# A megakernel's mixing stage: partition halves that hold row pairs, a projection in 64x64 quarters, one residual sum a pair, and x1 in DRAM at a padded channel pitch

## What is computed

```python
# layer 0
y = gn(x)                                  # group norm, 16 groups
qkv = dwconv3x3(conv1x1(y))                # 144 channels
q, k, v = blocks(qkv)                      # 8 heads x 96 rows (6 channels x 4x4 sites) x 16384 tokens
attn = softmax(normalise(q) @ normalise(k).T * temperature)   # 96 x 96 a head
x1 = x + proj(from_blocks(attn @ v))       # proj: 48x48, 1x1 conv
# layer 1: four recurrent sweeps (down, up, right, left), each step
#   next = line + conv1d_5(carry) + bias
out = x1 + sweeps(gn(x1))
```

## Time and profile before

| What | Value |
|---|---|
| median of 3 runs | 10475.02 us (10473.13 to 10499.15) |
| span of the profiled execution, first to last instruction | 10449.6 us |
| granted TensorE clock, mean | 0.956 |
| busy, share of the span: PE, PEld, DVE, ACT, POOL | 90%, 87%, 77%, 61%, 29% |
| mixing, first group's store to last group's store | 4142.0 to 5260.9 us |
| final sum, first to last addition | 9754.0 to 10435.6 us |

### The profile page before, as it was taken

The page is one execution under the profiler, slowest core; times in us unless marked ns, Lnnn a source line. Parts: engine busy times, 40 slices in busy tenths (PEclk is TensorE's granted clock), DMA queues, the critical chain, the costliest instruction groups (busy, mean ns, idle before and its releaser), DMA issues. The chain is left out here.

```text
span 10449.6 us, 213663 instructions
## 1 busy us (share of the span) xinstructions
PE 9389.1 (90%) x72744; PEld 9047.4 (87%) x72744; DVE 8070.5 (77%) x16201; ACT 6339.0 (61%) x11047; POOL 2982.2 (29%) x4333
## 2 busy tenths in 40 slices
PE   2999999999999998999979999999999999999100
PEld 2999999999999998777779999999999999999100
DVE  7888888777777776998977777777799997777333
ACT  2777777767777775444456667999833336666100
POOL 0000000000000000000046666666666666666100
PEclk9999999999999998999989999999999999999555
DMA  8888887666666666999968887777766657777899
GB/s 246 166 167 164 167 166 144 125 125 130 133 129 133 132 131 127 270 266 256 267 156 198 199 202 185 211 217 214 208 209 213 220 194 190 198 197 204 346 431 406
DMA packets 740412, 2101.28 MB, mean 201 GB/s; under 512 B 58480, under 2 KB 633232, under 8 KB 649184
## 3 DMA queue, kind: packets, MB, share of 16 engines
q1 hardware_dynamic: 611920, 1744.17, 65.5%
q10 hardware_dynamic: 106368, 204.76, 6.1%
q0 software_dynamic: 22016, 151.01, 5.9%
HBM read 1344.51 MB, written 754.97 MB: 201 GB/s over the span
## 5 line engine op out<-in xcount | busy, mean ns | idle before, releaser
L1448 ACT CAST hi<-rough 112x256 fp32r<-112x256 f32 x4096 | 1666.8, 407 | 1410.8 <-DVE rough L1362 1359.8
L1282 PE MATMUL scan_ps<-hi,scan_high 112*112 112x256 f32 x12264 | 2125.0, 282 | 30.6 <-ACT hi L1448 30.6
L1362 DVE SCALAR_TENSOR_TENSOR rough<-scan_ps,scan_bias,lines 112x256 f32<-112x256 f32 x4086 | 2136.3, 523 | 19.0 <-issue 14.4
L1293 PE MATMUL scan_ps_low<-lo,scan_high 112*112 112x256 f32 x12264 | 2130.5, 282 | 1.1 <-POOL lo L1394 0.7
L1288 PE MATMUL scan_ps_low<-hi,scan_low 112*112 112x256 f32 x12264 | 2123.3, 281 | 0.0
L438 PE MATMUL conv_ps<-tap_high,x_high 128*128 128x432 f32 (+2 forms) x6144 | 1884.0, 307 | 27.6 <-DVE vt L645 15.7
L438 PE MATMUL conv_ps<-tap_low,x_high 128*128 128x432 f32 (+2 forms) x6144 | 1908.3, 311 | 0.0
L438 PE MATMUL conv_ps<-tap_high,x_low 128*128 128x432 f32 (+2 forms) x6144 | 1905.1, 310 | 0.0
L1282 PEld LDWEIGHTS scan_ps<-hi,scan_high 112*112 112x112 f32 x12264 | 1691.3, 175 | 32.1 <-ACT hi L1448 31.3
L1293 PEld LDWEIGHTS scan_ps_low<-lo,scan_high 112*112 112x112 f32 x12264 | 1684.7, 175 | 5.6 <-POOL lo L1394 2.8
L1288 PEld LDWEIGHTS scan_ps_low<-hi,scan_low 112*112 112x112 f32 x12264 | 1687.1, 176 | 0.0
(11 more groups left out here) (140 smaller groups left out, 12398.8 us busy)
## 6 DMA issues: line engine op xcount, KB each, us to landing
raw<-x SPq DMA_DIRECT2D x764, 256.0 KB, 5.3
d_rows<-lines SPq DMA_DIRECT2D x32, 3584.0 KB, 30.2
u_cols<-lines SPq DMA_DIRECT2D x64, 1792.0 KB, 13.3
r_cols<-lines SPq DMA_DIRECT2D x32, 3584.0 KB, 24.3
lines<-u_cols SPq DMA_DIRECT2D x31, 3584.0 KB, 16.5
lines<-r_cols SPq DMA_DIRECT2D x30, 3584.0 KB, 16.6
lines<-d_rows SPq DMA_DIRECT2D x30, 3360.0 KB, 15.6
v_blocks<-xs ACTq DMA_DIRECT2D x128, 768.0 KB, 5.6
```

Of the source, the lines that this page charges most:

```text
L1282: last = nc.tensor.matmul(ps[:, b, 0:LP], high[:, shift], hi[:, b, (k - 1) % 2, shift:shift + LP], start=shift == 0, stop=shift == 2)
L1293: last = nc.tensor.matmul(ps_low[:, b, 0:LP], high[:, shift], lo[:, b, shift:shift + LP], start=False, stop=shift == 2)
L1362: nc.vector.scalar_tensor_tensor(rough[:, b, k % 2], ps[:, b, 0:LP], bias, line(way, s, k % T, b, kept), ALU.add, ALU.add).then_inc(rough_ ...
L1448: nc.scalar.copy(hi[:, b, k % 2, 1:LP + 1], rough[:, b, k % 2]).then_inc(hi_ready[b], 1)
```

## The change

The turned pair of sites now lies differently. `attT` is permuted by a new constant matrix `order` (the 8 transposes of the setup become 8 matmuls with `order_sb`), so that the two partition halves of `turned` hold an upper and a lower row of one block (dy and dy + 2), at one column dx. For odd dx the two halves are swapped. A pair is now one row parity `low` and two columns.

- Project: instead of 2 matmuls of 112x112 with 512 moving, a pair takes 4 of 48 x 64 or 48 x 48, each on one half of the rows and one half of the output columns of the array. The fourth pair of a group is projected one block later than before (`project(1 - s if i else s, i - 1 if i else N - 1)`), and the group's last turn moves behind the next group's first products.
- Sum: `res` has the same halves, so one addition of 112 x 1024 takes the place of four of 48 x 512. The bn_stats come four after every second pair instead of two after each; their number and size stay.
- `res` is loaded in runs of 4 KiB instead of 16 KiB, `scan_t` stored in runs of 8 KiB instead of 16 KiB; bytes and number of DMAs stay. A memset of `res` takes the place of that of `scan_t`, and the first loads of `res` wait for it.
- x1_scan is `[B, C, PITCH]`, 1 MiB + 4 KiB a channel. The down sweep's tiles are loaded as before (16 KiB a partition, four DMAs), with rows in another order inside a tile (`x1_row`).
- Because of the pad, `final_sum` loads x1 by four DMAs of 32 partitions x 32 KiB (one channel each) instead of one of 128 partitions, and adds in 8 operations of 128 x 1024 instead of four of 128 x 2048.

```diff
+RUN = T * W
+PITCH = G * RUN + 1024
...
+def x1_groups(x1_scan, b):
+
+    return x1_scan[b, :, 0:G * RUN].rearrange("c (g q f t w) -> c g q f t w", g=G, q=2, f=2, t=NP)
+
+
+def x1_row(t):
+
+    return NP * (t % N // 2) + 2 * (t // N) + t % 2
...
-    x1_scan = dram("x1_scan", (B, C, G, 2, T, W2))
+    x1_scan = dram("x1_scan", (B, C, PITCH))
...
         def load_res(queue, b, g, s, half):
-            queue.dma_start(res[ODD * half:ODD * half + C, s],
-                            x[b, :, bass.ds(T * g + NP * half, NP)]).then_inc(res_landed[half][s], 16)
-
-        def store(queue, b, g, s, q):
+            rows = x[b].rearrange("c (g i f l) w -> c g i f (l w)", g=G, i=NB, f=2)
+            queue.dma_start(res[ODD * half:ODD * half + C, s].rearrange("p (i l) w -> p i (l w)", i=NB),
+                            rows[:, bass.ds(g, 1), :, half].rearrange("c g i lw -> c (g i) lw")).then_inc(res_landed[half][s], 16)
+
+        def store(queue, b, g, s, half):
 
             queue.wait_ge(summed, N * G * b + N * g + N)
-            queue.dma_start(x1_scan[b, :, bass.ds(g, 1), q].rearrange("c g t w -> c (g t) w"),
-                            scan_t[ODD * q:ODD * q + C, s]).then_inc(scan_out[q][s], 16)
+            queue.dma_start(x1_groups(x1_scan, b)[:, bass.ds(g, 1), :, half].rearrange("c g q t w -> c (g q) (t w)"),
+                            scan_t[ODD * half:ODD * half + C, s].rearrange("p q t w -> p q (t w)")).then_inc(scan_out[half][s], 16)
...
+                sp.wait_ge(res_clear, 1)
...
-                nc.gpsimd.memset(scan_t[:], 0.0).then_inc(scan_clear, 1)
+                nc.gpsimd.memset(res[:], 0.0).then_inc(res_clear, 1)
+                pool.wait_ge(res_clear, 1)
...
-                        last = nc.tensor.transpose(w_ps[:, h // 4, (h % 4) * HD:(h % 4 + 1) * HD], diag[:, h], eye[0:HD, 0:HD])
+                        last = nc.tensor.matmul(w_ps[:, h // 4, (h % 4) * HD:(h % 4 + 1) * HD], diag[:, h], order_sb[:],
+                                                start=True, stop=True)
...
-                def project(j, s, ms, first):
-                    for m in ms:
-                        if not (first and m < NBANK):
-
-                            pe.wait_ge(summed, N * j + m // 2 - 1)
-                        nc.tensor.matmul(o_ps[:, m % NBANK], projd[:], flat(turned[:, s, m]),
-                                         start=True, stop=True).then_inc(o_done, 1)
-
-                def turn(n, slot, first):
+                def project(s, pair):
+                    for m in (2 * pair, 2 * pair + 1):
+                        for half in range(2):
+                            to = half if m % 2 == 0 else 1 - half
+                            wide = C if to else ODD
+                            last = nc.tensor.matmul(o_ps[ODD * to:ODD * to + wide, m % NBANK],
+                                                    projd[ODD * half:ODD * half + C, 0:wide],
+                                                    flat(turned[ODD * half:ODD * half + C, s, m]), start=True, stop=True)
+                    last.then_inc(o_done, 1)
...
-                        if not first:
-                            if i == 0:
-                                if second:
-                                    pe.wait_ge(proj_in, 32)
-
-                                pe.wait_ge(turn_moved, n)
-                            project(j - 1, 1 - s, (2 * i, 2 * i + 1), second)
-                    turn(NB * j + NB - 1, (NB - 1) % 2, False)
...
+                def group(b, j, s):
+                    for i in range(NB):
+                        products(b, j, s, i)
+
+                        pe.wait_ge(summed, N * j + i - 6)
+                        turn(NB * j + i - 1, (i - 1) % 2)
+                        project(1 - s if i else s, i - 1 if i else N - 1)
...
+                    bank, low, col = 2 * (pair % 2), pair // 2, 2 * (pair % 2)
+                    v.wait_ge(o_done, N * j + pair + 1)
+                    nc.vector.tensor_tensor(
+                        scan_t[:, s, :, low:NP:2, col // 2:W2:2],
+                        o_ps[:, bank:bank + 2].rearrange("p q (i j) -> p q i j", j=TOK),
+                        res[:, s, low:NP:2].rearrange("p i (j m) -> p m i j", m=N)[:, col:col + 2],
+                        ALU.add).then_inc(summed, 1)
+
+                def stats(b, g, s, low, last):
+                    j = G * b + g
+
+                    v.wait_ge(summed, N * j + 2 * low + 2)
+                    for q in range(2):
+                        for half in range(2):
+                            ins = nc.vector.bn_stats(x1_stats[:, b, bass.ds(NP * g + 4 * low + 2 * q + half, 1), :],
+                                                     scan_t[:, s, q, N * half + low:N * half + N:2])
...
+                return arriving(way, s).rearrange("p (b t n) -> p b t n", b=B, t=T)[:, b, x1_row(k)]
...
-                                x1_scan[b, :, bass.ds(g, 1), q].rearrange("c g t n -> c (g t n)")
+                                x1_groups(x1_scan, b)[:, bass.ds(g, 1), q].rearrange("c g f t n -> c (g f t n)")
...
-                    sp.dma_start(xt[:, s].rearrange("p q t w -> p (q t w)"),
-                                 x_runs[bass.ds(j, 1)].rearrange("j p f -> (j p) f")).then_inc(x_in[s], 16)
+                    for a in range(CPF):
+                        sp.dma_start(xt[G * a:G * (a + 1), s].rearrange("p q f t w -> p (q f t w)"),
+                                     x_runs[bass.ds(j, 1), a, 0:G * RUN].rearrange("j (g f) -> (j g) f", g=G)).then_inc(x_in[s], 16)
...
-                            ins = nc.vector.tensor_tensor(
-                                o_t[:, s, r:T:2, q:W:2].rearrange("p h (c m) -> p h c m", m=NP),
-                                xt[:, s, q, r:T:2].rearrange("p h (c m) -> p h c m", m=NP),
-                                lt[:, s, r, :, :, q:T:2].rearrange("p c h m -> p h c m"), ALU.add)
+                            for f in range(2):
+                                ins = nc.vector.tensor_tensor(
+                                    o_t[:, s, r + 2 * f:T:N, q:W:2].rearrange("p i (c m) -> p i c m", m=NP),
+                                    xt[:, s, q, f, r:NP:2].rearrange("p i (c m) -> p i c m", m=NP),
+                                    lt[:, s, r, :, f:NP:2, q:T:2].rearrange("p c i m -> p i c m"), ALU.add)
```

More of the change, by code:

```diff
@@ L763, in attention_weights_and_mix @@
         summed, stats_done = sem("summed"), sem("stats_done")
-        scan_out = [[sem(f"scan_{half}_out{s}") for s in range(2)] for half in ("even", "odd")]
+        scan_out = [[sem(f"scan_{half}_out{s}") for s in range(2)] for half in ("lower", "upper")]
         def batch_of(j):
@@ L911, in _, with products @@
-                for b in range(B):
-                    group(b, b * G, 0, first=b == 0)
-                    group(b, b * G + 1, 1, second=b == 0)
+                def products(b, j, s, i, first=False):
+                    n = NB * j + i
+                    if i == 0:
+                        pe.wait_ge(v_landed[s], 8 * (j - s) + 16)
+                    if not first:
+                        pe.wait_ge(taken, n)
+                    for h in range(HEADS):
+                        last = nc.tensor.matmul(a_ps[:, h // 4, (h % 4) * HD:(h % 4 + 1) * HD], v_in[:, s, h, i, :],
+                                                attT[:, b, h], start=True, stop=True)
+                    last.then_inc(att_done, 1)
@@ new lines, in start_of @@
+                def start_of(b):
+                    for i in range(NB):
+                        products(b, 0, 0, i, first=i == 0)
+                        if i:
+                            turn(i - 1, (i - 1) % 2, first=i == 1)
+                    for i in range(NB):
+                        products(b, 1, 1, i)
+                        if i > 2:
+                            pe.wait_ge(summed, i - 2)
+                        turn(NB + i - 1, (i - 1) % 2)
+                        if i == 1:
+                            pe.wait_ge(proj_in, 32)
+                        if i:
+                            project(0, i - 1)
@@ L916, in _ @@
                         group(b, b * G + 2 * i + 1, 1)
+                pe.wait_ge(summed, N * GROUPS - 6)
+                turn(NB * GROUPS - 1, (NB - 1) % 2)
+                project(0, N - 1)
                 pe.wait_ge(turn_moved, NB * GROUPS)
-                project(GROUPS - 1, 1, range(NM), False)
+                for pair in range(N):
+                    pe.wait_ge(summed, N * (GROUPS - 1) + pair - 1)
+                    project(1, pair)
             @block.scalar
@@ L1005, in _, with sums @@
                                           w_ps[:, :, 0:4 * HD]).then_inc(att_ready, 1)
[L1007 to L1009 removed]
+                def sums(b, g, s, pair):
                     j = G * b + g
[L1011 to L1029 removed]
@@ L1037, in whole @@
                             v.wait_ge(scan_out[half][s], 8 * (j - s))
-                    for dy in range(N):
```

(13 more changed lines are left out.)

71 lines of the change are left out of this document (26 added, 45 removed).

## The result

The change makes the kernel slower: 10760.6 us median against 10474.7, a ratio of 1.0296 (95% interval 1.0271 to 1.0321). The two medians alone give 1.0273; one of the four runs took 10865.3 us. The forecast of 10788 us lies 27 us above that. The profiled execution has a span of 10750.0 us, 300.4 more than before.

What follows compares the result with a forecast made beforehand. PE was taken to pace mixing with DMA close behind, and DMA alone to bind the final sum. Span 10449.6 + 133 (project) + 180 (final sum) = 10762.6, plus 25.4 gives 10788 us; range 10390 to 10960.

Steps and rivals of the forecast that it cites:

- Project, +133: Mixing on PE: staggered quarters and one exposed weight load make a group 19.8 us against 17.76, +133 us for 64 groups.
- The lower bound (0.86): Project in mixing: if all four quarters run at once, a pair takes 0.86 us.
- quarters at once, slower final sum: Rival for mixing and final sum: -93 + 180 us, total 10562 us; chance 0.12.
- DMA's floor: Mixing: loads and stores need at least 16.3 us a group, hidden at the forecast PE value.
- the gain of 93 us: Mixing bound: with quarters at once, DMA ends a group at 16.3 us instead of 17.76, -93 us for 64 groups.
- The sums: Mixing on DVE: 1.22 us a sum, 10.0 us a group, 14.9 at double time; hidden under PE, so no gain.
- The turn moved behind the next group's products: Mixing, at a group's end: the wait for ACT's copies adds nothing at the forecast project value.
- the fast case: Mixing with quarters at once: PE waits 1.4 us a group for ACT, so a group takes 15.4 us instead of 14.0.
- an exposed weight load: Project in mixing: one of two weight loads a block not hidden under matmuls, 0.18 us (bounds 0 and 0.35).
- The pad and the runs: DMA of mixing: the pad saves at most 1.1 us a group, hidden; shorter runs could cost part of that back.
- The final sum, +180: Final sum's x1 loads: 32 partitions at 200 GB/s take 11.2 us more; +7.5 us a round, 24 rounds, +180 us.
- I let a third be filled: Final sum: output stores fill a third of the slower loads' extra time, leaving +7.5 us a round.

Runs made afterwards that it cites:

- quick sums: The first kernel with columns 0 and 2 (then 1 and 3) of each four in a project pair: 10383.0 us, ratio 0.9923 to the kernel before.
- half of v: The first kernel loading only the first four heads' tiles of v, read twice: 10363.3 us, ratio 0.9907 to the kernel before.
- the first kernel: The changed kernel with the pad spread behind each 32 KiB run and the final x1 load one DMA of 128 partitions: 10480.4 us, ratio 1.0001 to the kernel before.
- the eighth kernel: The first kernel with the sum reading `res` in the order in which it lies: 10382.6 us, ratio 0.9925 to the kernel before.

## Why the forecast was right in sum and wrong in its steps

*Project, +133.* Wrong. The step that failed is "if PE starts in order, each further quarter can overlap only the second recording of the one before". The quarters run at once, 1.02 us instead of 2.33. The lower bound (0.86) was within 0.16 of the truth, and the sentence from the Trainium skill that I set beside it was the better guide. This was named as the rival "quarters at once, slower final sum", with 0.12.

*DMA's floor.* 16.3 us a group was near: with quick sums the stores come 16.8 us apart, with DMA at a share of 1.02 and 288 GB/s in the window shown, at which 4.72 MB take 16.4 us. The 16.36 us with half of v are no test of it, since they move less and PE needs 16.3 itself. That next to nothing of the gain of 93 us came in the change itself has another cause, next; with quick sums the ratio of 0.9923 is some 81 us.

*The sums.* The step that failed is "at double the time the sum is 14.9, still under PE. So this gives nothing while PE or DMA ends the block". The price was written down rightly as the bound (2.078 us is 1.7 times 1.22), and the conclusion was wrong. I compared the busy time of DVE with a group and found slack, in a stage where a load lands a whole group after its issue and arrives late now and then. Slack there isn't spare; it is what takes up lateness. The Trainium skill's rule on SBUF lines, quoted above, would have told me before the run that the upper bound was the value to take; I hadn't set it beside the new step of `res`. It cost about as much as the quick PE gave: ratio 1.0001 with slow sums, 0.9923 with quick ones.

*The clock.* Not in the forecast at all. In the earlier trace rows it is 1.00 and 0.98; from 4142 to 5200 us it is 0.96 in the changed kernel and 0.93 in the first. After a wait of PE it fell to 1.2 GHz in some cases, for three blocks in the stretch shown and more often for one.

*The turn moved behind the next group's products.* In the fast case I expected a wait for ACT of 1.4 us a group; it is 0.85, some 0.5 less. That a group takes PE 16.3 us and not the 15.4 forecast for this case comes from the blocks: 0.10 and 0.10 of products and turn and 0.16 of project, four times a group, are 1.4 us more. The same excess is all that the trace leaves room for where I took 0.18 us for an exposed weight load.

*The pad and the runs.* "So the pad can save at most 1.1 us", and it was counted as hidden. Nothing was found between a channel pitch of 1 MiB + 4 KiB and one of 1 MiB. "Shorter runs (4 and 8 KiB) could cost part of that back" isn't borne out for the loads: in the changed order of mixing the longer ones cost. For the stores it wasn't tried.

*The final sum, +180.* The slower loads were right, the size of the term wrong. The rate was 213 GB/s where I took 200. The error is "I let a third be filled": a round grew by 13.0 us, all of the estimated 11.2 and more. The rate alone gives 9.9 us of it. Stores of the output can't fill the gap, since the engines count as busy (share 1.01) while they hold the slow packets. Had I kept to the row that said 100% share, the term would have been 24 x 11.2 = +269, near the +300 measured.

*The total.* +133 +180 against -11 +12 +300. Two errors of opposite sign, one in each stage, made a good number. That is luck: with the quarters at once and nothing filled the same working gives 10475 - 93 + 269 = 10651, some 110 us too low. The slow sums, forecast as nothing and worth some 80 us by the ratios of the first and the eighth kernel, and 31 us more in the final sum are about the rest. The range and the chance of slower held because the final sum carried it alone.

## What to carry to other kernels

Before splitting a DMA, count the partitions that each piece covers: four loads of 32 partitions cost 300 us, four of 128 partitions and a quarter of the columns nothing. When an edit turns the order in which an engine reads a buffer, price the new step of every operand, and don't book slack of an engine as free when the transfers it waits for land about when they are needed: there, a shorter instruction pays although its engine isn't full. A stage that is slower than its longest resource is to be read by its late arrivals (who waited, and what the clock did after), not by its shares.

## What the runs showed of the hardware

- float32 matmuls of 48 rows x 48 or 64 columns on four quarters run at once: eight recordings from 4306.54 to 4307.56, 1.02 us, where four of 112x112 took 1.72.
- A float32 sum on 112 partitions, 1024 elements, one operand in PSUM: 1.229 us with the SBUF operand at every second element and the output contiguous, 1.232 with the operand contiguous and the output at every second, 2.078 with the operand at every fourth and the output at every second, 2.016 with the operand in neighbouring pairs of every four and the output alternating between two places 8 KiB apart. In the first and the last the PSUM reads alternate between two banks.
- Loads of 32 partitions hold the DMA engines at a share of 1.02 with 213 GB/s.
- After waits of PE of 1 us or more the granted clock fell to its lower level in some cases and not in others: 13 of 25 in the first kernel, 4 of 17 in the changed one. A block at that level took 7.30 us instead of 3.85.
- With loads of `res` in 16 KiB runs of 48 partitions this mixing was slower than with 4 KiB ones (ratios 1.0080 and 1.0001), though the kernel before loads in 16 KiB runs at 265 GB/s. Not explained.
